# Edge weights out of the histogram, 128-column weights, one scattered table and a paced last sum in a four-layer graph network kernel

## The reference

```python
h = relu(layernorm(x))
# layer 0: one attention score per edge (node, node and relation parts)
a = softmax of leaky_relu(z @ attn_w1 @ attn_w2) over each target's edges
x += relu(segment_sum(a * h[src], dst) + h @ loop_weight)      # h itself where a node has no edge
# layer 1: rows and columns, no weights
x += relu(concat[h, segment_sum(h[col] @ W_msg + b_msg, row)] @ W_upd + b_upd)
# layer 2: two rounds of weighted sums
deg = maximum(segment_sum(w, dst), 1);  norm = deg ** -0.5
h = segment_sum((h * norm)[src] * w, dst) * norm               # twice; mean of the three
# layer 3: 8 heads, self loops, softmax over each target's edges and its own score
e = leaky_relu(a_src[src] + a_dst[dst]);  alpha = softmax(e)
x += layernorm(ff(...)) of mean over heads of segment_sum(alpha * h[src], dst)
```

## Time and profile before

| | us |
|---|---|
| median of three runs | 5580.41 |
| the profiled execution | 5609.29 |
| its span in the profile | 5607.6 |
| PE busy in the span | 2765.6 (49%) |
| DVE busy | 2436.0 (43%) |
| PE's weight loads | 2175.0 (39%) |
| POOL busy | 1797.6 (32%) |
| ACT busy | 473.0 (8%) |

### The profile page before, as it was taken

One profiled execution on the slowest core, in us unless ns is written; L12 is line 12 of the kernel. 1 busy time (PEld: TensorE's weight loads), 2 busy tenths in 40 slices (PEclk: granted clock), 3 DMA queues, 4 the chain that ended last, 5 costly groups with the idle time before them and its releaser, 6 DMA issues.

```text
span 5607.6 us, 46533 instructions
## 1 busy us (share of the span) xinstructions
PE 2765.6 (49%) x14416; PEld 2175.0 (39%) x14458; DVE 2436.0 (43%) x4207; ACT 473.0 (8%) x909; POOL 1797.6 (32%) x1742
## 2 busy tenths in 40 slices
...
GB/s 109 52 1 61 58 75 62 71 62 65 85 82 140 138 144 155 109 49 160 177 269 220 44 52 49 46 48 10 0 0 23 70 80 73 49 15 66 63 35 23
DMA packets 246489, 433.22 MB, mean 77 GB/s; under 512 B 140538, under 2 KB 142311, under 8 KB 231895
## 3 DMA queue, kind: packets, MB, share of 16 engines
...
q1 hardware_dynamic: 64102, 198.46, 10.0%
...
...
## 4 chain that ended last, share of the span: by engine, by line
PE 35%; issue 25%; another core or an unknown queue 17%; DVE 10%; POOL 9%; DMA 2%; ACT 1%; DVEq 0%; SPq 0%; ACTq 0%; POOLq 0%
POOL ring L652 8%; PE PS L1272 7%; PE PS L1196 5%; PE PS L1096 4%; PE PS L1098 4%; PE PS L989 3%; PE PS L1029 3%; PE PS L1167 3%; PE PS L992 2%; PE PS L1175 1%; DVE s_ring L1612 1%; DVE s_ring L1613 1%; PE PS L1270 1%; PE PS L1290 1%
## 5 line engine op out<-in xcount | busy, mean ns | idle before, releaser
L652 POOL DMA_INDIRECT ring<-d_h,idx_lin x1568 | 1579.1, 1007 | 598.6 <-issue 519.4
L1272 PE MATMUL PS<-arena,s_ring 128*128 x1968 | 432.5, 414 | 198.1 <-issue 198.1
L1096 PE MATMUL PS<-qa 128*125 128x150 bf16 x1050 | 412.3, 393 | 107.0 <-DVE arena L1662 46.1
L1929 DVE TENSOR_TENSOR big<-PS,big 128x800 f32<-128x800 f32 x196 | 193.8, 989 | 619.5 <-issue 335.7
L1272 PEld LDWEIGHTS PS<-arena,s_ring 128*128 128x128 f32 x1968 | 439.8, 330 | 9.2 <-issue 1.1
L1221 PE MATMUL PS<-big 128*125 128x128 bf16 x784 | 134.0, 300 | 618.5 <-issue 449.2
L1098 PE MATMUL PS<-qa 128*125 128x150 bf16 x1050 | 401.2, 382 | 0.0
L1059 PE MATMUL PS<-s_ring,arena 81*128 81x512 bf16 x196 | 121.6, 621 | 561.0 <-issue 353.3
L1221 PEld LDWEIGHTS PS<-big 128*125 128x125 bf16 x784 | 106.9, 209 | 664.8 <-issue 456.6
L671 POOL DMA_INDIRECT d_fa<-asd,start_i x25 | 50.2, 2010 | 889.5 <-DVEq L1323 882.2
L1231 PE MATMUL PS<-big,arena 125*128 125x200 bf16 x2352 | 271.6, 272 | 118.3 <-ACT arena L900 100.9
...
## 6 DMA issues: line engine op xcount, KB each, us to landing
big<-d_wgt SPq DMA_DIRECT2D x50, 1562.5 KB, 7.2
d_stash<-ring SPq DMA_DIRECT2D x196, 256.0 KB
arena<-d_stash ACTq DMA_DIRECT2D x196, 256.0 KB
big<-d_cnt SPq DMA_DIRECT2D x25, 1562.5 KB, 6.5
ring<-d_h,idx_lin POOLq DMA_INDIRECT x1568
d_cnt<-big ACTq DMA_DIRECT2D x13, 1562.5 KB, 5.5
d_wgt<-big ACTq DMA_DIRECT2D x13, 1562.5 KB, 15.7
d_cnt<-arena ACTq DMA_DIRECT2D x12, 1562.5 KB, 5.4
```

The costliest lines, as they stand in the source:

```text
L652: pool.indirect_dma_start(ring[:, HALF * h + s, :], None, table, bass.IndirectOffsetOnAxis(ap=idx_lin[:, CH * i + s:CH * i + s + 1], axis= ...
L1096: nc.tensor.matmul(bank(3 * half + s // 2, NP, 2 * CW, at), lhs, hot_step(half, s, W, 2 * CW), start=(s % 2 == 0), stop=False, skip_group_ ...
L1272: mm = nc.tensor.matmul(PS[:, bass.ds(place[s] + j % SUMS * BANK, D)], marks[:, j % 2, s, :], arena[:, bass.ds(at[s], D)], start=False, st ...
L1929: v_.tensor_tensor(picked.rearrange("p (s h k) -> p s h k", s=CB, h=H), free(PS[:, 0:1], [[BANK // 2, CB], [NB, H], [1, NB]], 2 * j * BANK ...
```

## The change

Five things change together.

1. **Histogram.** The products with the edge weights are gone: `w3` and its setup, DVE's third operation of a round, and three of the four column groups of PE's moving operand. The weight sums come in another way: SP stores the weights in edge order (`d_wl`) and loads them back (`w_edge`); after layer 0's softmax DVE makes a segmented running sum (`scan_one`), SP stores it (`d_wsum`), and POOL gathers each node's last value into `norm` with 25 gathers. DVE waits for them ahead of layer 2.
2. **Weight columns.** W becomes 128 in the histogram and in the builder (both the parts and the overflow), so their one-hot operands have 128 columns in place of 125 (126 written). The score lookup of layer 3 keeps 126 under the name LKW.
3. **Order of the transfers.** The first gather sequence stops at chunk 94; the last 32 gathers stand behind those of `d_al0`. SP's store of `d_al0` moves into `stash(0)` at chunk 94. In layer 3 the `self_rows` stand at the end.
4. **One scattered table.** `d_fa3` is twice as wide and takes the targets' and own scores together (25 scatters of 16 values); `d_fb3` is gone. `softmax3` fills in four quarters.
5. **Layer-3 sums.** A table `chunks_for` tells each round how many chunks it needs. PE loads the number and waits for `chunks_seen`, which ACT raises after waiting for each chunk. After the 2nd, 4th and 6th tile of a round PE multiplies ones by 512 columns, into a bank that nobody reads, as in layer 0's sums.

```diff
-    W = NP + 1
+    W = P
+    LKW = NP + 1
...
+        ALPHA_AT = 94
+        ROWS_AT, LATE = 57, 60
...
+                    if turn == 0 and i == ALPHA_AT:
+                        sp.wait_ge(S["blk_ready"], NB)
+                        sp.wait_ge(S["dense_out"], 32)
+                        sp.wait_ge(S["fill_in"], 16)
+                        sp.dma_start(w_edge, d_wl.rearrange("(p c) k -> p (c k)", p=P)).then_inc(S["fill_in"], 16)
+                        sp.wait_ge(S["alpha_ready"], 1)
+                        sp.dma_start(d_al0.rearrange("(p c) k -> p (c k)", p=P), qa[:, 0:C]).then_inc(S["alpha_out"], 16)
...
             stash(0)
 
-            sp.wait_ge(S["alpha_ready"], 1)
-            sp.dma_start(d_al0.rearrange("(p c) k -> p (c k)", p=P), qa[:, 0:C]).then_inc(S["alpha_out"], 16)
-
             sp.wait_ge(S["blk_out0"], 32 * (NB // 2 + 2))
             sp.wait_ge(S["blk_out1"], 32 * (NB // 2 + 1))
             sp.wait_ge(S["alpha_out"], 16)
+            sp.wait_ge(S["alpha_ready"], 2)
+            sp.dma_start(d_wsum.rearrange("(p c) k -> p (c k)", p=P), w_sum).then_inc(S["alpha_out"], 16)
...
-            tiles(0, d_h0, 40, NCH)
+            tiles(0, d_h0, 40, ALPHA_AT)
             pool.wait_ge(S["alpha_out"], 16)
             block_rows(d_al0, alpha0, "rows_in")
+            tiles(0, d_h0, ALPHA_AT, NCH)
 
             dst_rows = d_dst.rearrange("(t e) k -> t (e k)", e=P)
             for g in range(G16):
                 n = rows16(g)
                 pool.indirect_dma_start(dst16[0:n, g * P:(g + 1) * P], None, dst_rows,
                                         bass.IndirectOffsetOnAxis(ap=tk16_i[0:n, g:g + 1], axis=0)).then_inc(S["rows16_in"], 16)
+            pool.wait_ge(S["alpha_out"], 32)
+            for b in range(NB):
+                pool.indirect_dma_start(norm[:, b:b + 1], None, d_wsum, bass.IndirectOffsetOnAxis(ap=last_i[:, b:b + 1], axis=0),
+                                        bounds_check=EP - 1, oob_is_err=False).then_inc(S["nodes_in"], 16)
 
             pool.wait_ge(S["asd_sb"], 1)
-            to_starts(d_fa3, lambda b: asd[:, b, H:2 * H], "fill_out")
-            to_starts(d_fb3, lambda b: packed(nself, H)[:, b, :], "own_out")
+            to_starts(d_fa3, lambda b: both[:, b, :], "fill_out")
             pool.wait_ge(S["h3_out"], 16)
             tiles(1, d_h3, 0, ROWS_AT)
-            pool.wait_ge(S["alpha_out"], 16 * 2)
+            pool.wait_ge(S["alpha_out"], 16 * 3)
             alpha_rows = d_al3.rearrange("(t e) k -> t (e k)", e=P)
             for g in range(G16):
                 n = rows16(g)
                 pool.indirect_dma_start(al_rows[0:n, g * P * H:(g + 1) * P * H], None, alpha_rows,
                                         bass.IndirectOffsetOnAxis(ap=tk16_i[0:n, g:g + 1], axis=0)).then_inc(S["rows_in"], 16)
-            tiles(1, d_h3, ROWS_AT, SELF_AT)
+            tiles(1, d_h3, ROWS_AT, NCH)
             pool.wait_ge(S["nmx_ready"], 1)
             pool.wait_ge(S["scan_out"], 16)
             self_rows(d_sum3, packed(nmx, H))
-            tiles(1, d_h3, SELF_AT, NCH)
...
+            seen = [0]
+
+            def see(n):
+
+                while seen[0] < n:
+                    act.wait_ge(S[f"chunk_in{seen[0] % 4}"], chunk_count(1, seen[0]))
+                    act.sem_inc(S["chunks_seen"], 1)
+                    seen[0] += 1
+
             for c in range(PREFILL):
                 reload(1, c, SLOTS, "step_mm", 0)
+                see(c - 2)
             for u in range(AL_UNITS):
                 act.wait_ge(S["rows_tr"], R_SB + u + 1)
                 to, n = al_cols(u)
                 nc.scalar.activation(to, bank(u % 8, P, n), ACT.Copy).then_inc(S["rows_sb"], 1)
             for c in range(PREFILL, NCH):
                 reload(1, c, SLOTS, "step_mm", c - 2)
+                see(c + 1 if c >= LATE else c - 1)
...
-                mm = nc.tensor.matmul(bank(7, NP, 4 * NB), free(s_bf[:, 0:1], [[HALF, NP]], h * W * HALF + s_),
-                                      free(h_bf[:, 0:1], [[HW * HALF, 4], [HALF, NB]], h * 4 * HW * HALF + s_),
+                mm = nc.tensor.matmul(bank(7, W, NB), free(s_bf[:, 0:1], [[HALF, W]], h * W * HALF + s_),
+                                      free(h_bf[:, 0:1], [[HALF, NB]], h * HW * HALF + s_),
                                       start=(c == 0), stop=(c == C - 1))
...
-                    lhs = hot_step(half, s, 0, NP)
-                    nc.tensor.matmul(bank(3 * half + s // 2, NP, 2 * CW, at), lhs, hot_step(half, s, W, 2 * CW),
+                    lhs = hot_step(half, s, 0, W)
+                    nc.tensor.matmul(bank(3 * half + s // 2, W, 2 * CW, at), lhs, hot_step(half, s, W, 2 * CW),
                                      start=(s % 2 == 0), stop=False, skip_group_check=True)
-                    mm = nc.tensor.matmul(bank(3 * half + s // 2, NP, 2 * CW, at + CW), lhs, hot_step(half, s, W + 2 * CW, 2 * CW),
+                    mm = nc.tensor.matmul(bank(3 * half + s // 2, W, 2 * CW, at + CW), lhs, hot_step(half, s, W + 2 * CW, 2 * CW),
                                           start=False, stop=False, skip_group_check=True)
...
-                if j < NCH:
-                    pe.wait_ge(S[f"chunk_in{j % 4}"], chunk_count(1, j))
                 pe.wait_ge(S["marks_ready"], j + 1)
+                chunks = pe.value_load(chunks_for[:, j:j + 1], min_val=1, max_val=NCH)
                 at = nc.values_load_multi_w_load_instructions(
                     slot_at[:, j * CH:(j + 1) * CH], engines=[mybir.EngineType.PE], min_val=0, max_val=(SLOTS * CH - 1) * D,
                     skip_runtime_bounds_check_because="a step's slot is a tile's number modulo the slots")[1]
@@ -1267,10 +1300,13 @@
                     skip_runtime_bounds_check_because="a window is at most one behind the window of the step before it")[1]
                 if j >= SUMS:
                     pe.wait_ge(S["step_added"], j - SUMS + 1)
+                pe.wait_ge(S["chunks_seen"], chunks)
                 nc.tensor.matmul(bank(j % SUMS, P, BANK), zero_bf[:, 0:P], zero_bf[:], start=True, stop=True)
                 for s in range(CH):
                     mm = nc.tensor.matmul(PS[:, bass.ds(place[s] + j % SUMS * BANK, D)], marks[:, j % 2, s, :], arena[:, bass.ds(at[s], D)],
                                           start=False, stop=False, skip_group_check=True)
+                    if s % 2 and s < CH - 1:
+                        nc.tensor.matmul(bank(6, P, BANK), ones_bf[:, 0:P], free(ones_bf[:, 0:1], [[0, 2], [1, 2 * P]]), start=True, stop=True)
                 mm.then_inc(S["step_mm"], 1)
...
-            for j in range(3):
-                go(v_.tensor_copy(w3[:, j, :], w_lin))
-                if j < 2:
-                    go(v_.tensor_tensor(w_lin, w_lin, w3[:, j, :], ALU.subtract))
...
-            w_at = free(w3[:, 0, 0:1], [[C, 3], [0, HW], [1, C]])
             iota_d = iota_h.rearrange("p (c s) -> p c s", s=HALF)
             for i in range(C // HALF):
                 h, c = i % 2, i * HALF
                 v.wait_ge(S["hist_used"], HALF * (i + 1))
-                hot_d = free(h_bf[:, 0:1], [[HALF, HW], [1, HALF]], h * 4 * HW * HALF)
+                hot_d = free(h_bf[:, 0:1], [[HALF, HW], [1, HALF]], h * HW * HALF)
                 v_.tensor_tensor(free(s_bf[:, 0:1], [[HALF, W], [1, HALF]], h * W * HALF), iota_d, dlo_at[:, :, c:c + HALF], ALU.is_equal)
-                go(v_.tensor_tensor(hot_d, iota_d[:, 0:HW, :], dhi_at[:, :, c:c + HALF], ALU.is_equal))
-                v_.tensor_tensor(free(h_bf[:, 0:1], [[HW * HALF, 3], [HALF, HW], [1, HALF]], (h * 4 + 1) * HW * HALF),
-                                 free(h_bf[:, 0:1], [[0, 3], [HALF, HW], [1, HALF]], h * 4 * HW * HALF),
-                                 w_at[:, :, :, c:c + HALF], ALU.mult).then_inc(S["hist_s"], 1)
...
+                for r in range(4):
+                    first, buf = r * C4, fill_buf[r % 2]
+                    if r == 3:
+                        v.wait_ge(S["self_in"], 16)
+                    else:
+                        v.wait_ge(S["fill_in"], 16 * (4 + r // 2))
                     for j in range(H):
-                        go(v_.tensor_tensor_scan(free(sm[:, 0:1], [[H, C2]], h * C2 * H + j), notst[:, h * C2:(h + 1) * C2], free(fa_half[h][:, 0:1], [[H, C2]], j),
-                                                 sm[:, (C2 - 1) * H + j:(C2 - 1) * H + j + 1] if h else 0.0, *SUMOP), False)
-                    v.wait_ge(S["dve"], done[0])
+                        go(v_.tensor_tensor_scan(free(sm[:, 0:1], [[H, C4]], first * H + j), notst[:, first:first + C4], free(buf[:, 0:1], [[2 * H, C4]], j),
+                                                 sm[:, (first - 1) * H + j:(first - 1) * H + j + 1] if r else 0.0, *SUMOP), False)
+                    go(v_.scalar_tensor_tensor(free(own[:, 0:1], [[H, C4], [1, H]], first * H), free(notst[:, 0:1], [[1, C4], [0, H]], first), -BIG,
```

(7 more changed lines are left out.)

103 lines of the change are left out of this document (55 added, 48 removed).

## The result

The changed kernel took 5625.29 us in the median of 7 runs (5605.35 to 5655.82), the kernel before 5580.41 beside it (5571.78 to 5598.33). The ratio is 1.0074, 95% interval 1.0049 to 1.0098: it is slower by 45 us (0.7%, small but clear of 1 by its interval) where 107 us of gain was forecast, and the time lies above the range. The profiled execution of the change, 5606.31 us, is at the fast end of its runs, and the profiled one of before (5609.29) lies 11 us above the slowest of those seven.

A forecast was written before the change was run, and what follows sets the result against it. PE was taken to bound the builder, sums and histogram, with late PE results beside dense gathers. Terms -4 - 73 - 36 + 3 - 55 + 80 - 9 + 3 - 16 = -107 gave a 5473 us median; range 5390 to 5580.

The forecast's parts named there:

- Step 8: Layer-3 sums: matmuls of ones raise the clock to 1.00, 3.63 us a round; -16 us (-30 to +20).
- rival A: Layer-3 sums: the clock stays low, a round takes 5.1 us instead of 3.85, +150; 5639 us, chance 0.12.
- Step 5: Layer 0's sums: 72 gathers one behind the other delay PE's results for 86 us; +80 us (0 to +95).
- hold: Beside back-to-back POOL gathers, each PE matmul's result comes 2.8 us late, until some 20 us after they end.
- rival C: Layer 0's sums: the gathers beside them don't delay PE, so no +80; 5393 us, chance 0.15.
- Step 2: Histogram rounds behind the gathers: faster loads, fewer moving columns, 0.98 us a round instead of 1.84; -73 us.
- Rival B: Histogram and builder: strided 128-column loads are no faster, giving -33 and 0; 5568 us, chance 0.16.
- Step 4: Builder: faster loads end PE's limit, the store of weights then bounds at 20.1 us a block; -55 us.
- Steps 1, 3, 6 and 7: Histogram setup -4 us; score lookup -36 and +3; look stage -9; softmax of layer 3 +3.

The follow-up runs named there:

- e2: The changed kernel with a fourth matmul of ones in each round of the layer-3 sums; 5501.22 us, 0.9867 of the kernel before.
- g1: e2 with the 32 tile gathers again ahead of layer 0's softmax and the weight sums' gathers behind layer 0's sums; 5442.18 us, ratio 0.9752.
- f3: The changed kernel with 75 in place of 150 moving columns in the builder's matmuls; 3777.57 us, in a session kind where the kernel before took 3781 to 3792.

## Why the prediction was wrong, by its steps

**Step 8 failed, by its clock.** The prediction said that three ones and the zeroing one make the mix alike to layer 0's. It was alike in count of 512-column matmuls, and the clock stayed at 0.50: rival A, given 0.12. Its price was 5.1 us a round and came out at 4.69, the 0.34 us of the load in it; beside the gathers five slow rounds of 55 us followed the first, where six of 47 stood. So the stage, from the first bank added to the last, grew by 96 us, where -16 was written and A had said +150. That alone turns a kernel 107 us faster into one about as fast; in the table, whose stage begins a little earlier, this row is 119 us off. e2 shows that one matmul more would have made the step true in its clock. The step's round of 3.63 us was right for that clock (3.58 measured).

**Step 8's load had the right size.** 0.6 for two rounds was taken, 0.68 measured (0.34 a round). The wait that it replaces was worth 0, as said, in the held kind; in the free kind the exchange was worth 90 us.

**Step 5 was right, its hold in part by luck.** +80 was forecast, +73 profiled, 246.6 against 326.2 in g1; rival C fell where it was judged. But C describes this stage of the free kind, with 248.7 us. The hold was taken to last 86 us, until 20 us behind the last gather. It lasted 81: results came late from 2074 us on, and the first row behind the hold is

```profile
2155.51 4.68 DVE L1888 TENSOR_SCALAR s_ring<-iota_row,arena 128x125 f32<-128x125 f32 x18 [3.15 <-PE PS L1022]
```

only 2 us behind the last gather's end (2153.06). The gathers themselves took 98 us and not 92, since those of the weight sums come every 1.57 us and not 1.28. The two misses nearly cancel.

**Step 2 was right, its size short** (-91 for -73). A round takes 0.82 us, less than the 0.98 taken: DVE is busy throughout, its two operations (0.692 and 0.259 us) overlap, and nothing is handed over late. The load's gain holds for the strided operand, 164 ns for 326. Rival B fell for the histogram (it needed more than 1.3 us a round); in the builder, where B said 0, the gain of 12 us is near to it, though the loads did get faster.

**Step 4 failed as well, by what it took for the limit.** The reasoning took the load for what spaced the builder's matmuls, so that PE would stop being the limit. It was the 150 moving columns (f3: 0.204 to 0.104 us), so PE stayed the limit and the step gave -12 for -55. The row was there to be read: these loads took 250 ns, the matmuls came every 204, so the loads overlapped with other work and didn't set the spacing. Nor would the store have bounded at 20.1 us a block, as f3 ran at 19.4.

**Steps 1, 3, 6 and 7** came within 13 us each (-4, -41, -22, +3); what made the look stage 13 us shorter than forecast was not traced. That the time came near to no change at all is luck in part: the misses of step 8 and of the builder, 119 and 43 us, stand against 58 us by which all other rows of the table together came out below their forecast.

The two profiles differ by -3 us and the medians by +45, so 48 us are in no row of the table, for the reason given at the top. Layer 0's sums, whose clock rises sooner or later, can hold up to 28 of them (352.6 against 324.9); that they do is not shown.
